# Partner rows land in three buffers and are added on VectorE, with the expert layers' gathers ordered by blocks of three

## The chip, the cores and the metric

The kernel runs on one core of one Trainium2 chip. The metric is the time of one launch on the device in microseconds (us). Engines are called PE (TensorE), DVE (VectorE), ACT (ScalarE), POOL (GpSimd) and SP (SyncE); PEld is PE's weight load. "Clock" is the TensorE clock that the chip granted, 1.0 being 2.4 GHz and 0.5 being 1.2 GHz.

## The reference, cut to what matters

Four layers follow each other on x of 4 x 1024 tokens of 128 numbers, each as `x = x + layernorm(layer(layernorm(x)))`: an attention over channels, a ternary feed-forward layer, a 16-head attention, and two expert layers. The change touches the last of them alone:

```python
xg = x.reshape(bsz, 4, n, d)...reshape(4, S, d)       # 4 groups of S = 1024 tokens
def per_group(xf, lw, lb):                            # E = 24 experts, top 2, C = 86 places
    combine, dispatch = top2_dispatch(xf, Wg, C)
    h = moe_apply(xf, combine, dispatch, W1, b1)      # 128 -> 512, a token's two experts summed
    h = relu(layer_norm(h, lw, lb))
    return moe_apply(h, combine, dispatch, W2, b2)    # 512 -> 128, summed again
return layer_norm(out + x, ln_out_w, ln_out_b)
```

A token sits in one place of each of its two experts. Its hidden row is the sum of two rows, one from each place, so each place needs the row of its partner place, and the token's result is again the sum of the rows at its two places.

## The kernel before, in words

The kernel is one program with its order written out by hand for each engine. Up to about 826 us of the profile stand the other layers; `expert_layers` is the rest. Work goes by group h (0 to 3). A group has 18 tiles of 128 places, in 6 blocks (NB) of 3 tiles (TPB) and 4 experts each. A block is numbered m or n, 0 to 23 over all groups; below, "block 2 of group 1" is m = 8.

The steps of a block are these.

- **Input.** POOL gathers token rows by index into one of the input buffers `XS` (`gather_x`, three gathers of 128 rows of 512 bytes). PE turns them (`x_transposes`, tile e_px), ACT copies (`xt`), PE multiplies by W1 (`up`, tile e_ph), ACT scales by the gate into `HS` (`hidden`, tile e_hs), and SP stores the three tiles to `h_rows` in HBM (`h_store`).
- **Partner.** When all 18 tiles of a group are stored (`h_out`), POOL gathers each tile's partner rows, 128 rows of 2 KB, and the DMA adds them onto `HS` in flight (`partners`, `ALU.add`).
- **Norm and second product.** ACT sums squares and takes the root (`std`), DVE scales the three tiles (`normed`), PE turns them in four chunks (`h_transposes`, tile e_pn), ACT applies relu into `HT` (`relu`), PE multiplies by W2 (`down`, tile e_py), DVE scales the result into `YS` (`result`) and SP stores it to `y_rows` (`y_store`).
- **Output.** Once a group's six results are stored, POOL gathers 16 tiles of result rows, 512 bytes each, into `YA` (`results`), and DVE adds them, normalises twice and adds to x (`output`); SP stores x (`x_store`).

While a group's second products run, PE also runs the first products of the next group: `beside(m)` puts one `up` behind each of the group's first four blocks, two behind the fifth and none behind the sixth. The last group has none. An `up(n)` starts with the transposes of block n+1. `pY` has two banks, so `down(m)` waits for `result(m-2)`.

Every gather goes through `gather`, which lets four be in flight: gather k waits for k-4 to have landed. `STAGES` numbers them in the order in which POOL issues them, and `landed` is how others wait for one. In group 0, DVE also works out the places of groups 2 and 3 (`choice.…`), with products on PE between its blocks (`map_products` behind `up(6)` and `up(7)`, which wait for `choice.spread`; `last_products` behind them, which wait for `choice.map_rows`).

The change touches `place` and `STAGES` (L1078 to L1088), the loops of SP, POOL, PE, ACT and DVE in `expert_layers` (L1713 to L2116), and the buffers at its head.

Of the kernel before, what the change touches and what calls it, by code (L numbers as in the profile page):

```python
# [13 lines left out]
P = 128  # L14
# [959 lines left out]
def exact_maxima(nc, R, S):  # L974

    with ExitStack() as ctx:
# [56 lines left out]
        def _(pe):  # L1033
# [39 lines left out]
NXS = 4  # L1073
# [4 lines left out]
STAGES = (("x", 0, 0), ("x", 0, 1), ("x", 1, 0), ("h", 0, 0), ("x", 1, 1), ("x", 2, 0), ("h", 1, 0), ("x", 2, 1), ("y", 0, 0),  # L1078
          ("x", 3, 0), ("h", 2, 0), ("x", 3, 1), ("y", 1, 0), ("h", 3, 0), ("y", 2, 0), ("y", 3, 0))
LENGTH = {"x": NT // 2, "h": NT, "y": 2 * GT}  # L1080
# [3 lines left out]
def place(stage, h, j):  # L1084

    if stage == "x":
        return FIRST[stage, h, 2 * j // NT] + j % (NT // 2)
    return FIRST[stage, h, 0] + j  # L1088
# [624 lines left out]
def expert_layers(nc, R, A, DR):  # L1713

    with ExitStack() as ctx:
# [8 lines left out]
        HT = [sb(f"e_ht{c}", [P, TPB * P]) for c in range(FC)]  # L1724
# [18 lines left out]
         sq_done, std_done, ov_done, od_done, out_done) = (sem("e_" + n) for n in (  # L1743
             "xt_mm", "xt_done", "h_mm", "hs_done", "n_done", "hn_mm", "ht_done", "y_mm", "ys_done",
             "ya_read", "o_done", "sq_done", "std_done", "ov_done", "od_done", "out_done"))
# [15 lines left out]
        def _(sp):  # L1761
# [12 lines left out]
            def x_store(h):  # L1774
                sp.wait_ge(o_done, h + 1)
                for b in range(B):
# [9 lines left out]
            for m in range(NU):  # L1786
                for n in beside(m):
                    h_store(n)
                y_store(m)
                if m == 3:  # L1790
# [7 lines left out]
                if m % NB == NB - 1 and m >= NB:  # L1798
                    x_store(m // NB - 1)
            x_store(GR - 1)  # L1800
# [3 lines left out]
        def _(pool):  # L1804
            token_numbers(nc, pool, R, W, 1)

            def inputs(h, first):
                pool.wait_ge(R["rows_done"], h + 1)
                if h == 2:
                    pool.wait_ge(R["x_out"], 16 * HB)  # L1810
                for n in range(h * NB + 3 * first, h * NB + 3 * first + 3):
                    if n >= NXS:
                        pool.wait_ge(xt_mm, n - NXS + 1)
                        gather_x(nc, R, n)

            def partners(h):
# [5 lines left out]
            def results(h):  # L1822
                for i in range(2):
                    pool.wait_ge(ys_out[i], (h + 1) * NB // 2 * 16)
                if h >= 1:
                    pool.wait_ge(ya_read, 2 * h)
                else:
                    pool.wait_ge(R["rows_done"], GR)
                for i in range(GT):
# [3 lines left out]

            inputs(0, 0)
            inputs(0, 1)
            inputs(1, 0)
            partners(0)
            inputs(1, 1)
            inputs(2, 0)
            partners(1)  # L1840
            inputs(2, 1)
            results(0)
            inputs(3, 0)
            partners(2)
            inputs(3, 1)
            results(1)
            partners(3)
            results(2)
            results(3)

        @block.tensor
        def _(pe):
# [11 lines left out]
            def up(n):  # L1864
                if n + 1 < NU:
# [26 lines left out]
            def down(m, c):  # L1892
# [10 lines left out]
                for e in range(EB):  # L1903
                    last = mm(out[0:ROWS, e * D:(e + 1) * D], HT[c][:, e * ROWS:(e + 1) * ROWS], W2[:, eb * EB + e, c, :],  # L1904
# [16 lines left out]
            for m in range(NU):  # L1921
                if m % NB == 0:
                    for c in range(FC):
                        h_transposes(m, c)
                for c in range(FC):
                    down(m, c)
                    if m % NB < NB - 1:
# [11 lines left out]
        def _(act):  # L1939
# [6 lines left out]
            def hidden(n):  # L1946
                if n + 1 < NU:
# [9 lines left out]
            def std(m):  # L1957
                for t in range(m * TPB, (m + 1) * TPB):
                    landed(act, R, place("h", t // NT, t % NT))
# [9 lines left out]
            def relu(m):  # L1969
                h = m // NB  # L1970
                for c in range(FC):
                    k = FC * m + c
                    act.wait_ge(hn_mm, k + 1)
                    if m >= 1:
                        act.wait_ge(y_mm, FC * (m - 1) + c + 1)
                    src = pN[k % 2][:, 0:TPB * P].rearrange("p (j s) -> p j s", j=TPB)
                    for cols, slots in ((slice(0, TPB * ROWS), slice(0, ROWS)), (slice(TPB * ROWS, EB * ROWS), slice(ROWS, P))):
                        r = nc.scalar.activation(HT[c][:, cols].rearrange("p (j s) -> p j s", j=TPB), src[:, :, slots],  # L1978
# [9 lines left out]
            for h in range(GR):  # L1988
# [4 lines left out]
                for j in range(NB):  # L1993
                    if j < 3:
                        std(m + j + (2, 2, 3)[j])
                    if j < NB - 1:
                        relu(m + j + 1)
                    if j == 1:
                        std(m + 4)
                    for n in beside(m + j):  # L2000
                        hidden(n)
            for n, eps in enumerate((R["c_ln_eps"], R["c_eps"])):
                act.wait_ge(ov_done, n + 1)
                nc.scalar.activation(or1, ov, ACT.Sqrt, bias=eps, scale=1.0 / D).then_inc(od_done, 1)

        @block.vector
        def _(v):
# [3 lines left out]
            group = lambda ap, h: ap.rearrange("p (b h r) d -> p b h r d", b=B, h=GR)[:, :, h, :, :]  # L2011

# [17 lines left out]
            def normalise(h, eps):  # L2030
                for i in range(GT):
                    c.mark(nc.vector.bn_stats(sto[:, i, :], Yn[:, i // 2 * TB + 2 * h + i % 2, :]))  # L2032
                c.wait()
                last = finish_stats(nc, c, sto, omean, ov, ot1, ot2, D)
                if h < GR - 1:
                    c.run(last)
                    rsqrt(nc, c, ov, or1, ot1, 1.0 / D, eps)
                else:
                    last.then_inc(ov_done, 1)
                    v.wait_ge(od_done, 1 if eps == LN_EPS else 2)  # L2040
                    c.run(nc.vector.reciprocal(or1, or1))
                for i in range(GT):
# [4 lines left out]
            def output(h):  # L2047
# [179 lines left out]
```

## Time and profile before

| | us |
|---|---|
| median of 3 runs (lowest, highest) | 1206.05 (1205.61, 1211.87) |
| profiled execution: its own time | 1214.45 |
| profiled execution: span | 1212.7 |
| busy in the span: PE, ACT, DVE, POOL | 910.2, 793.9, 562.8, 378.3 |
| expert layers, from 826 us to the end | about 387 |

From 800 us on no engine is busy throughout: PE is 45 of 50 us in 800 to 850, but 25.69 of 50 in 1000 to 1050 and 24.86 of 50 in 1100 to 1150. So what matters there is who waits for whom. The chain that ended last gives this: it is followed back from the last instruction, at each step to what released it. A timeline gives each instruction's start, its length, and in brackets the idle time of its engine before it with what ended it. Where several instructions stand on one line, "x3" counts them.

### The profile page before, as it was taken

The page shows a single profiled execution, that of the slowest core. Times are in us where ns is not written, and L with a number is a line of the kernel's source. Part 1 is how long each engine was busy: PE and PEld are TensorE (multiplying, and loading weights), DVE is VectorE, ACT ScalarE, POOL GpSimd, SP SyncE. Part 2 cuts the span into 40 slices and gives each one's busy share as a digit, 9 for nine tenths or more (in the row PEclk, how much of TensorE's full clock was granted, in tenths as well). Part 3 has the DMA queues.
Part 4 walks back from the last instruction along what each step waited for, and adds up shares of the span by engine and source line. Part 5 has one row for each costly group of instructions (what it writes and reads, how often), then busy time and mean ns, then how long its engine had stood idle before and what let it go on. Part 6 is the DMA issues. An engine that isn't in the chain of part 4 may idle for free. (4 is left out here: it accounts for less than half of the span.)

```text
span 1212.7 us, 18733 instructions
## 1 busy us (share of the span) xinstructions
PE 910.2 (75%) x6570; PEld 431.7 (36%) x6570; DVE 562.8 (46%) x1894; ACT 793.9 (65%) x1181; POOL 378.3 (31%) x333
## 2 busy tenths in 40 slices
PE   4746974661599999999999999998499496594740
PEld 4633762330122222222222223323276364463640
DVE  7488767894001444344445153334351225326356
ACT  2133351453699999999999999994476483574720
POOL 6222442543300000000000000115572766866752
PEclk9657996886699999999999999998699698698875
DMA  3000005647921111111112121238786874966821
GB/s 98 1 1 1 1 1 129 162 114 203 324 78 49 52 46 61 52 61 52 61 52 62 53 61 30 64 79 238 163 167 198 136 175 127 169 173 142 154 68 50
DMA packets 83615, 118.37 MB, mean 98 GB/s; under 512 B 8974, under 2 KB 45583, under 8 KB 83410
## 3 DMA queue, kind: packets, MB, share of 16 engines
q1 hardware_dynamic: 67344, 88.72, 24.2%
q0 software_dynamic: 14752, 27.81, 13.6%
q10 hardware_dynamic: 1442, 0.86, 0.3%
q8 instruction: 43, 0.70, 0.3%
q14 instruction: 34, 0.28, 0.1%
HBM read 72.66 MB, written 44.70 MB: 97 GB/s over the span
## 5 line engine op out<-in xcount | busy, mean ns | idle before, releaser
L1466 ACT ACTIVATE s_e<-s_ps 128x1024 f32<-128x1024 f32 x512 | 486.9, 1025 | 30.0 <-PE s_ps L1615 29.4
L1628 PE MATMUL s_acc<-s_e,s_v 128*32 128x512 f32 x2048 | 274.5, 608 | 0.1
L1615 PE MATMUL s_ps<-s_q,s_k 64*128 64x512 bf16 x1024 | 196.0, 389 | 50.2 <-ACT s_e L1466 22.6
L1100 POOL DMA_INDIRECT x_in<-x_tokens,rows_of x72 | 70.2, 976 | 502.2 <-DVE rows_of L1259 456.0
L1615 PEld LDWEIGHTS s_ps<-s_q,s_k 64*128 64x128 bf16 x1024 | 49.2, 93 | 320.7 <-ACT s_e L1466 274.8
L1100 POOL DMA_INDIRECT e_hs<-h_rows,rows_of x72 | 116.3, 1615 | 65.0 <-DMA h_rows<-e_hs 42.0
L1888 PE MATMUL e_pn<-ident,e_hs 128*128 128x128 f32 x288 | 54.1, 307 | 78.4 <-DVE e_hs L2018 57.3
L1904 PE MATMUL e_py<-w,e_ht 128*96 128x128 f32 x768 | 103.0, 282 | 0.0
L1978 ACT ACTIVATE e_ht<-e_pn,ln_hid 128x288 f32<-128x288 f32 x192 | 84.8, 507 | 26.7 <-PE e_pn L1888 26.7
L1904 PEld LDWEIGHTS e_py<-w,e_ht 128*96 128x96 f32 x768 | 92.5, 170 | 0.0
L1962 ACT ACTIVATE l_so<-e_hs 128x512 f32<-128x512 f32 x72 | 45.2, 628 | 65.1 <-DMA e_hs<-h_rows,rows_of 62.4
L1874 PE MATMUL e_ph<-w,e_xt 128*32 128x512 f32 x576 | 78.3, 617 | 5.7 <-ACT e_hs L1954 5.7
L1100 POOL DMA_INDIRECT e_ya<-y_rows,take x64 | 62.8, 981 | 27.6 <-issue 18.8
L1954 ACT ACTIVATE e_hs<-e_ph,gate_of 128x512 f32<-128x512 f32 x72 | 49.2, 687 | 31.0 <-PE e_ph L1877 30.3
L1888 PEld LDWEIGHTS e_pn<-ident,e_hs 128*128 128x128 f32 x288 | 38.3, 158 | 83.4 <-DVE e_hs L2018 44.4
L1548 DVE COPY s_as<-s_acc 128x512 f32<-128x512 f32 x32 | 22.1, 689 | 90.0 <-PE s_acc L1628 90.0
L1628 PEld LDWEIGHTS s_acc<-s_e,s_v 128*32 128x32 f32 x2048 | 40.4, 108 | 59.8 <-issue 56.0
L1566 DVE RECIPROCAL s_rec<-s_px 128x16 f32<-128x16 f32 x32 | 8.2, 258 | 114.8 <-PE s_px L1639 114.7
L2026 DVE TENSOR_TENSOR e_ys<-e_py,gate 96x512 f32<-96x512 f32 x24 | 16.3, 684 | 67.3 <-PE e_py L1904 67.3
L2016 DVE RECIPROCAL gate_exponents<-gate_exponents 128x3 f32<-128x3 f32 x24 | 4.2, 175 | 92.4 <-ACT gate_exponents L1966 92.4
L618 PE MATMUL f_pu<-f_zt,up_t 128*128 128x512 f32 x64 | 33.8, 663 | 9.8 <-ACT f_h L486 9.8
L500 POOL TENSOR_TENSOR f_sq<-f_sq 128x1024 f32<-128x1024 f32 x8 | 18.9, 2357 | 54.9 <-DVE f_sq L544 54.9
(413 smaller groups left out, 1334.9 us busy)
## 6 DMA issues: line engine op xcount, KB each, us to landing
h_rows<-e_hs SPq DMA_DIRECT2D x72, 256.0 KB, 3.1
s_k<-stack_k SPq DMA_DIRECT2D x32, 512.0 KB, 4.5
s_q<-stack_q SPq DMA_DIRECT2D x32, 256.0 KB, 3.2
w<-in_w SPq DMA_DIRECT2D x1, 6144.0 KB, 21.7
y_rows<-e_ys SPq DMA_DIRECT2D x24, 192.0 KB
stack_q<-b_parts SPq DMA_DIRECT2D x8, 384.0 KB, 4.5
stack_k<-b_parts SPq DMA_DIRECT2D x6, 384.0 KB, 4.3
x_res<-in_x SPq DMA_DIRECT2D x4, 512.0 KB, 7.3
```

What stands on the lines that cost most here:

```text
L618: mm(pU[f % 2][:], R["up_t"][:, f * P:(f + 1) * P], ZT[:, k * CH:(k + 1) * CH], start=True, stop=True).then_inc(up_mm, 1)
L1100: nc.gpsimd.indirect_dma_start(dst, None, rows, bass.IndirectOffsetOnAxis(ap=idx, axis=0), compute_op=op).then_inc(R["landed"][k % FLIGHT] ...
L1466: nc.scalar.activation(E[g % 4][:, 2 * pair:2 * pair + 2, :], pS[pair][:].rearrange("p (a s) -> p a s", a=2), ACT.Exp, scale=SCALE).then_i ...
L1548: nc.vector.tensor_copy(AS[hu % 2][:], acc[hu % 2][:]).then_inc(acc_read, 1)
L1615: last = nc.tensor.matmul(pS[pair][:, a * CH:(a + 1) * CH], K[c % 2][rows, pair, j * P:(j + 1) * P], Q[c % 2][rows, pair, :], start=True, ...
L1628: last = nc.tensor.matmul(acc[hu % 2][32 * h:32 * h + 32, :], V4[c % 2][:, j, h, :], E[g % 4][:, h, :], start=j == 0, stop=j == TB - 1)
L1874: mm(pH[m % 2][32 * q:32 * q + 32, :], XT[n % 2][:, j * P + 32 * q:j * P + 32 * q + 32], W1[:, e, :], start=True, stop=False)
L1888: tr = nc.tensor.transpose(pN[k % 2][:, j * P:(j + 1) * P], HS[:, m % NB * TPB + j, c * P:(c + 1) * P], ident[:])
L1904: last = mm(out[0:ROWS, e * D:(e + 1) * D], HT[c][:, e * ROWS:(e + 1) * ROWS], W2[:, eb * EB + e, c, :], start=False, stop=c == FC - 1, sk ...
L1954: nc.scalar.activation(HS[:, m % NT, :], pH[m % 2][:], ACT.Copy, scale=G128[:, n // NB, m % NT:m % NT + 1]).then_inc(hs_done, 1)
L1962: nc.scalar.activation(squares, HS[:, t % NT, :], ACT.Square, accum_out=ssq[:, t % NT:t % NT + 1]).then_inc(sq_done, 1)
L1978: r = nc.scalar.activation(HT[c][:, cols].rearrange("p (j s) -> p j s", j=TPB), src[:, :, slots], ACT.Relu, bias=lnh[:, 1, h, c:c + 1], sc ...
```

## The change

Six things change together. **Gathers of partner rows** no longer add: they land in one of three buffers `GA` (tile l_o, which is the old buffer `O`, and two new ones named e_ga), and DVE adds the buffer onto `HS` (`added`, one 128x512 addition a tile). A gather waits until the buffer's last addition is done. **POOL's order** goes by blocks: partner blocks and input blocks alternate after the first three partner blocks. **Input buffers** fall from four to three. **The transposes** of a group's first input block move from the last `up` of the group before to the start of the group, between `h_transposes` and `down` of its first block. **Results** are gathered, normalised and stored by halves of 4 tiles, and stand later: output of group 0 moves from group 1 to group 2, that of group 1 from group 2 to group 3, and that of group 2 from behind the last result to between the results of group 3. **ACT's** `std` and `relu` are reordered accordingly, and `std` waits for DVE's additions.

```diff
-NXS = 4
+NXS = 3
+NHT = 4
+NGA = 3
...
+        GA = [R["O"][:].rearrange("p t d -> p (t d)"), sb("e_ga1", [P, FF])[:], sb("e_ga2", [P, FF])[:]]
...
+            def partners(first, end):
+                h = first // NB
                 pool.wait_ge(h_out[h], 16 * NT)
-                for j in range(NT):
-                    gather(nc, R, place("h", h, j), HS[:, j, :], DR["h"][h].rearrange("t p f -> (t p) f"),
-                           IDX[:, h, 1, j:j + 1], ALU.add)
+                for j in range(first % NB * TPB, (end - h * NB) * TPB):
+                    t = h * NT + j
+                    if t < NGA:
+                        pool.wait_ge(R["late_mm"], (HB - 1) * NX + 1)
+                    else:
+                        pool.wait_ge(add_done, t - NGA + 1)
+                    gather(nc, R, place("h", h, j), GA[t % NGA], DR["h"][h].rearrange("t p f -> (t p) f"),
+                           IDX[:, h, 1, j:j + 1])
...
             def up(n):
-                if n + 1 < NU:
+                if n % NB < NB - 1:
                     x_transposes(n + 1)
...
             for m in range(NU):
-                if m % NB == 0:
+                h, j = m // NB, m % NB
+                if j == 0:
                     for c in range(FC):
                         h_transposes(m, c)
+                    if h + 1 < GR:
+                        x_transposes(m + NB)
...
+            def added(m):
+                for t in range(m * TPB, (m + 1) * TPB):
+                    landed(v, R, place("h", t // NT, t % NT))
+                    nc.vector.tensor_tensor(HS[:, t % NT, :], HS[:, t % NT, :], GA[t % NGA], ALU.add).then_inc(add_done, 1)
...
             for h in range(1, GR):
                 m = h * NB
-                for j in range(3):
-                    normed(m + j)
+                added(m)
+                added(m + 1)
+                normed(m)
+                added(m + 2)
+                normed(m + 1)
+                added(m + 3)
+                normed(m + 2)
                 result(m)
+                added(m + 4)
                 normed(m + 3)
                 result(m + 1)
+                added(m + 5)
                 normed(m + 4)
                 normed(m + 5)
+                if h == 3:
+                    output(1, 0)
                 for j in range(2, NB):
                     result(m + j)
-                    if j == 3 and h < GR - 1:
-                        output(h - 1)
-            output(GR - 2)
-            output(GR - 1)
+                    if h == 2 and j in (2, 4):
+                        output(0, j // 2 - 1)
+                    if h == 3 and j in (2, 4):
+                        output(j // 2, 2 - j // 2)
+            output(2, 1)
+            output(3, 0)
+            output(3, 1)
```

Three places show how instructions move; the prediction speaks of each.

DVE in group 0, before: from the last write of group 2's rows (`last_rows`, L1259) to the read of group 3's map (L1248). L1236 and L1238 are `spread(3)`, L2016 and L2018 `normed(3)`, L2026 `result(1)`.

```order
L1259 CAST rows_of<-e_pm 32x36
L1236 TENSOR_TENSOR v_all<-e_ya,v_all 128x1536
L1238 TENSOR_TENSOR v_all<-e_ya 128x1152
L2016 RECIPROCAL gate_exponents<-gate_exponents 128x3
L2018 TENSOR_SCALAR e_hs<-e_hs,gate_exponents 128x512 x3
L2026 TENSOR_TENSOR e_ys<-e_py,gate 96x512
L1248 COPY e_ya<-e_pm 96x72
```

The same place now; L2057 are the additions of blocks 4 and 5, L1242 and L1244 are `spread(3)`, L2072 is `result(1)`, L1254 reads the map.

```order
L1265 CAST rows_of<-e_pm 32x36
L2057 TENSOR_TENSOR e_hs<-e_hs,l_o 128x512
L2057 TENSOR_TENSOR e_hs<-e_hs,e_ga 128x512 x2
L1242 TENSOR_TENSOR v_all<-e_ya,v_all 128x1536
L1244 TENSOR_TENSOR v_all<-e_ya 128x1152
L2062 RECIPROCAL gate_exponents<-gate_exponents 128x3
L2064 TENSOR_SCALAR e_hs<-e_hs,gate_exponents 128x512 x3
L2057 TENSOR_TENSOR e_hs<-e_hs,l_o 128x512
L2057 TENSOR_TENSOR e_hs<-e_hs,e_ga 128x512 x2
L2072 TENSOR_TENSOR e_ys<-e_py,gate 96x512
L1254 COPY e_ya<-e_pm 96x72
```

The additions of block 5 now stand ahead of the map's read.

POOL from group 1's partners on, before: all 18 partner tiles in a row, then 9 tiles of input, 16 of results and 9 of input.

```order
L1100 DMA e_hs<-h_rows,rows_of 128x512 x18
L1100 DMA x_in<-x_tokens,rows_of 128x128 x9
L1100 DMA e_ya<-y_rows,take 128x128 x16
L1100 DMA x_in<-x_tokens,rows_of 128x128 x9
L1100 DMA e_hs<-h_rows,rows_of 128x512 x18
```

The end of group 1's stretch now, from its partner block 4 on; e_ya is half of group 0's results.

```order
L1106 DMA l_o<-h_rows,rows_of 128x512
L1106 DMA e_ga<-h_rows,rows_of 128x512 x2
L1106 DMA x_in<-x_tokens,rows_of 128x128 x3
L1106 DMA l_o<-h_rows,rows_of 128x512
L1106 DMA e_ga<-h_rows,rows_of 128x512 x2
L1106 DMA x_in<-x_tokens,rows_of 128x128 x6
L1106 DMA e_ya<-y_rows,take 128x128 x8
L1106 DMA x_in<-x_tokens,rows_of 128x128 x3
L1106 DMA l_o<-h_rows,rows_of 128x512
```

Partner gathers come in threes with three input gathers between them, and only 8 result gathers stand ahead of the next group.

DVE behind the last `normed` of group 3, before: the last four results (L2026) in a row, then the first additions of group 2's output (L2053, L2054).

```order
L2018 TENSOR_SCALAR e_hs<-e_hs,gate_exponents 128x512 x3
L2026 TENSOR_TENSOR e_ys<-e_py,gate 96x512 x4
L2053 TENSOR_TENSOR v_all<-v_all,e_ya 128x2x256
L2054 TENSOR_TENSOR v_all<-v_all,e_ya 128x2x256
L2053 TENSOR_TENSOR v_all<-v_all,e_ya 128x2x256
```

There now: the end of the first half of group 1's output, then block 2's result (L2072), then the start of the other half.

```order
L2092 TENSOR_SCALAR v_all<-v_all,gate_exponents 128x128 x4
L2112 TENSOR_TENSOR x_res<-x_res,v_all 128x2x256
L2072 TENSOR_TENSOR e_ys<-e_py,gate 96x512
L2101 TENSOR_TENSOR v_all<-v_all,e_ya 128x2x256
L2102 TENSOR_TENSOR v_all<-v_all,e_ya 128x2x256
L2080 BN_STATS gate_exponents<-v_all 128x6 x4
```

Each of block 2's to block 5's results now has a half of an output ahead of it or behind it.

## Rows read from the trace of the kernel before

**Rows 1.** chain that ended last, 740 to 1213 us, shares by line.
```profile
by line: POOL e_hs L1100 20.2%; issue 9.8%; PE e_ph L1874 7.9%; DMA e_hs<-h_rows,rows_of 6.7%; PE e_py L1904 6.5%; POOL e_ya L1100 6.2%; DMA h_rows<-e_hs 2.7%; DMA x_in<-x_tokens,rows_of 2.6%; PE e_pn L1888 2.4%; PE e_ph L1877 1.9%; PE e_px
```

**Rows 2.** timeline of POOL: start us, length us, line, what; idle before.
```profile
943.27 1.57 POOL L1100 DMA_INDIRECT e_hs<-h_rows,rows_of  x1 [17.73 <-DMA h_rows<-e_hs]
945.15 1.55 POOL L1100 DMA_INDIRECT e_hs<-h_rows,rows_of  x1 [0.30 <-issue]
1028.28 1.57 POOL L1100 DMA_INDIRECT e_hs<-h_rows,rows_of  x1 [5.27 <-DMA h_rows<-e_hs]
1105.78 1.57 POOL L1100 DMA_INDIRECT e_hs<-h_rows,rows_of  x1 [7.51 <-DMA h_rows<-e_hs]
```

**Rows 3.** timeline of ACT, group 1's start.
```profile
948.09 0.63 ACT L1962 ACTIVATE l_so<-e_hs 128x512 f32<-128x512 f32 x1 [9.46 <-DMA e_hs<-h_rows,rows_of]
959.57 1.70 ACT L1978 ACTIVATE e_ht<-e_pn,ln_hid 128x288 f32<-128x288 f32 x4
```

**Rows 4.** timeline of PE, group 1.
```profile
962.44 1.97 PE L1904 MATMUL e_py<-w,e_ht 128*96 128x128 f32 x8
1018.48 0.87 PE L1861 MATMUL e_px<-ident,x_in 128*128 128x128 f32 x3 [6.18 <-DMA x_in<-x_tokens,rows_of]
937.83 0.42 PE L1900 MATMUL e_py<-bias_split,expert_hot 128*96 128x128 bf16 x4
```

**Rows 5.** chain that ended last: PE's steady blocks, then two plain gathers landing.
```profile
916.67 0.90 PE e_py L1904 x8
925.54 0.90 PE e_py L1904 x8
1014.41 3.82 DMA x_in<-x_tokens,rows_of
1189.74 2.79 DMA e_ya<-y_rows,take
```

**Rows 6.** timeline of POOL, a plain gather of input rows.
```profile
1013.16 0.94 POOL L1100 DMA_INDIRECT x_in<-x_tokens,rows_of  x1 [0.30 <-issue]
```

**Rows 7.** timeline of DVE, scaling of three tiles.
```profile
953.99 1.28 DVE L2018 TENSOR_SCALAR e_hs<-e_hs,gate_exponents 128x512 f32<-128x512 f32 x3
```

**Rows 8.** windows: PE, PEld, DVE, ACT, POOL busy; PEclk, DMA share, GB/s.
```profile
950.00:956.00 6.00, 0.68 (x3) 0.68 (x4) 1.46 (x4) 2.46 (x7) 5.00 (x4) 0.50 0.87 136
```

**Rows 9.** timelines of PE and DVE in group 0.
```profile
873.88 1.51 PE L1888 MATMUL e_pn<-ident,e_hs 128*128 128x128 f32 x6 [13.50 <-DVE e_hs L2018]
907.37 0.42 PE L1900 MATMUL e_py<-bias_split,expert_hot 128*96 128x128 bf16 x4
884.78 1.74 DVE L1236 TENSOR_TENSOR v_all<-e_ya,v_all 128x1536 f32<-128x1536 f32 x1
886.45 1.34 DVE L1238 TENSOR_TENSOR v_all<-e_ya 128x1152 f32<-128x1152 bf16 x1
```

**Rows 10.** timelines of PE and DVE in group 3.
```profile
1123.13 1.54 PE L1888 MATMUL e_pn<-ident,e_hs 128*128 128x128 f32 x6 [17.67 <-DVE e_hs L2018]
1125.04 1.71 PE L1888 MATMUL e_pn<-ident,e_hs 128*128 128x128 f32 x6 [0.36 <-ACT e_ht L1978]
1139.44 0.69 DVE L2026 TENSOR_TENSOR e_ys<-e_py,gate 96x512 f32<-96x512 f32 x1 [0.79 <-PE e_py L1904]
```

**Rows 11.** timeline of DVE, last two output stages.
```profile
1168.61 1.64 DVE L2032 BATCH_NORM_STATS2 gate_exponents<-v_all 128x6 f32<-128x128 f32 x8
1173.65 2.14 DVE L2044 TENSOR_SCALAR v_all<-v_all,gate_exponents 128x128 f32<-128x128 f32 x8
1175.83 2.90 DVE L2060 TENSOR_TENSOR v_all<-v_all,gate_exponents 128x256 f32<-128x256 f32 x8
1186.06 1.23 DVE L2064 TENSOR_TENSOR x_res<-x_res,v_all 128x1024 f32<-128x1024 f32 x1
1192.65 0.69 DVE L2053 TENSOR_TENSOR v_all<-v_all,e_ya 128x512 f32<-128x512 f32 x1 [4.04 <-DMA e_ya<-y_rows,take]
1207.59 1.22 DVE L2064 TENSOR_TENSOR x_res<-x_res,v_all 128x1024 f32<-128x1024 f32 x1
```

More of the change, by code:

```diff
@@ L1772, in y_store, with x_store @@
                              ).then_inc(ys_out[m % 2], 16)
-            def x_store(h):
-                sp.wait_ge(o_done, h + 1)
-                for b in range(B):
+            def x_store(h, half):
+                sp.wait_ge(o_done, 2 * h + half + 1)
+                for b in range(2 * half, 2 * half + 2):
                     t = b * TB + 2 * h
@@ L1832, in results @@
                                take[:, h * GT + i, k:k + 1])
[L1834 to L1849, printed above, removed]
+            inputs(3, 9)
+            partners(0, 3)
+            inputs(9, 10)
+            partners(3, 4)
+            inputs(10, 11)
+            partners(4, 5)
+            inputs(11, 12)
+            partners(5, 6)
+            inputs(12, 15)
+            partners(6, 9)
+            inputs(15, 16)
+            partners(9, 10)
+            inputs(16, 17)
+            partners(10, 11)
+            inputs(17, 18)
+            partners(11, 12)
+            inputs(18, 20)
+            results(0, 0)
+            inputs(20, 21)
+            partners(12, 15)
+            inputs(21, 22)
+            partners(15, 16)
+            inputs(22, 23)
+            partners(16, 17)
+            inputs(23, 24)
+            partners(17, 18)
+            results(0, 1)
+            results(1, 0)
+            partners(18, 24)
+            results(1, 1)
+            for h in (2, 3):
+                results(h, 0)
+                results(h, 1)
         @block.tensor
@@ L1992, in _ @@
                 relu(m)
[L1993 to L1999, printed above, removed]
+                if h + 1 < GR:
+                    xt(m + NB)
+                for j in range(NB - 2):
+                    if j < 2:
+                        std(m + j + 2)
+                    relu(m + j + 1)
+                    if 1 <= j <= 2:
+                        std(m + j + 3)
                     for n in beside(m + j):
                         hidden(n)
-            for n, eps in enumerate((R["c_ln_eps"], R["c_eps"])):
-                act.wait_ge(ov_done, n + 1)
-                nc.scalar.activation(or1, ov, ACT.Sqrt, bias=eps, scale=1.0 / D).then_inc(od_done, 1)
+                relu(m + NB - 1)
+                for n in beside(m + NB - 2):
+                    hidden(n)
+            for half in range(2):
+                ts = slice(half * GT // 2, (half + 1) * GT // 2)
+                for n, eps in enumerate((R["c_ln_eps"], R["c_eps"])):
+                    act.wait_ge(ov_done, 2 * half + n + 1)
+                    nc.scalar.activation(or1[:, ts], ov[:, ts], ACT.Sqrt, bias=eps, scale=1.0 / D).then_inc(od_done, 1)
         @block.vector
```

112 lines of the change are left out of this document (60 added, 52 removed), and 3 rows, old and new, of the table STAGES.

## The prediction, written before the changed kernel had run

> **What bounds the kernel now.** I read the page's busy shares and slices first: behind 826 us no engine is full, so I turned to the chain that ended last for that stretch [rows 1]. A fifth of it is POOL writing the accumulating gathers (e_hs), 6.7% is their landing, the rest is PE work and the result gathers. The timelines show why. Each group has a handover: the last hidden tile is stored, POOL starts the partner gathers at 943.27, 1028.28 and 1105.78 in groups 1 to 3 [rows 2], and PE stands until the first blocks are normed. Call these starts G1, G2, G3. A group so lasts 85.0 us (G1 to G2), 77.5 (G2 to G3), and group 3 from G3 to the end of the span 106.9.
>
> **Prices.** An accumulating gather takes 1.55 us of POOL and 0.30 to the next [rows 2], and lands 4.8 us after its start (943.27 to ACT's 948.09) [rows 3]. A plain one of 512-byte rows takes 0.94 and 0.30 [rows 6] and lands 2.79 us after its start on a quiet chip, 3.82 beside other transfers [rows 5]. A plain gather of 2 KB rows is in no row. Its issue lies between 0.94 and 1.55; I take 0.95, since the number of rows is that of the plain ones and the accumulation is what goes. Its landing lies between 2.8 and 4.8; I take 3.3, half a microsecond above the quiet one for four times the bytes. A DVE addition of 128x512 is 0.69 [rows 11], about 0.72 apart. With three buffers, gather t+3 starts when t is added: 3.3 + 0.7 + 0.3 = 4.3 us a block, against 5.55 now. PE's steady block, second products and one `up`, is 8.87 us (916.67 to 925.54), the fifth block with two `up` 12.3 (to 937.83) [rows 4, 5].
>
> **Start of groups 1 to 3, from the gathers' start.** Now relu begins at +16.3 (959.57) [rows 3] and `down` of the first block at +19.2 (962.44) [rows 4]. Changed: third tile issued at 2.5, landed 5.8, added 6.5; block 1 added at 10.8. DVE has `added` of block 1 ahead of `normed` of block 0, so scaling (1.28 for three tiles [rows 7]) ends at 12.3. PE's transposes make relu possible at 13.3, `down` 2.9 later and 0.6 more for the moved input transposes: +16.8, a gain of 2.4.
>
> **Group 1.** `down` and `up` of the first block, as now 10.7 us, end at +27.5. POOL has per block three input gathers and three partner ones, 6 x 1.25 = 7.5 us, under PE's 8.87, but each input gather waits for transposes in the `up` three blocks earlier. Followed through: partner block 3 is added at +27, block 4 at +34.5. ACT has `std` of block 4 ahead of `hidden` of the second `up`, so that `up` loses 1.3. Block 5 is added at +43.3, in time within 0.2. So PE is at 27.5 + 3 x 8.87 + 1.5 = 55.6, the fifth block ends at +67.9, and 4.7 us later, as now, the next partner gathers start: 72.6 instead of 85.0. Of the 12.4 won, 2.4 is the start, 6.2 PE's wait for input rows at 1018.48, which stood behind 16 result gathers [rows 4], the rest small stalls of ACT. **Group 2** has the same sequence, and its outputs stand behind `added` and `normed`; the halves are hidden beside PE, whose two result banks suffice there. 72.6 against 77.5: 4.9 won.
>
> **Group 0 loses.** PE's first transposes are where they are now, 873.88 [rows 9]; with ACT not in the way the four chunks take 3.6 us as in group 3 (1123.13 to 1125.04 + 1.71) [rows 10], the input transposes 0.5: 878.0. Only then may POOL gather input block 9 (3.75 us) and behind it partner block 3: third tile started at +6.4, landed +9.7, added +10.5. DVE then does `normed(2)` (1.5) and `spread(2)` (3.1, [rows 9]), and `map_products` waits for that: it starts at 893.0 and PE gets to `down` of block 1 at 897. Second gate: the transposes of the following `up` end at 902.9, input block 11 and partner block 5 follow by the same 10.5, and DVE's map read stands behind `added` of block 5 and `result`: 914.4. `down` of block 2 starts at 915.2, now at 907.37 [rows 9]: 7.8 lost.
>
> **Group 3.** G3 is at 943.27 + 7.8 + 72.6 + 72.6 = 1096.2, 9.5 ahead of now. DVE comes 1.3 late to its additions, being in the last half of group 0's output. PE's first transposes are at +13.8, block 1's result 16.3 later (1123.13 to 1139.44) [rows 10], less 1.5 for stalls that go: +29; block 5 is added at 33 and the last `normed` ends at +36. From there DVE has no gap: four halves of output with the twelve-instruction root, five results of 0.7, two last halves. A whole stage now is 4 x 0.72 of additions, then 18.7 (1168.61 to 1186.06 + 1.23), of which 2 x 1.64 + 2 x 2.14 + 2.90 + 1.23 = 11.7 grows with the tiles [rows 11]. A half is 1.4 + 18.7 - 5.85 = 14.2; the small instructions aren't halved. The last group, with ACT's root, takes 16.2 from 1192.65 to 1208.8, so a half 16.2 - 5.85 = 10.4. Sum: 36.2 + 14.2 + 0.7 + 14.2 + 1.4 + 14.2 + 0.7 puts the last result at +81.6; its store and POOL's wake-up some 3.3 (as h_rows), eight gathers 10, landing: the second-last half could start at 96.5, and DVE is free at 95.8. So two halves of 10.4 end at +117.3, and the store takes the 3.9 of now (1208.8 to 1212.7): +121.2 against 106.9, 14.3 lost. PE isn't the bound: `down` of blocks 4 and 5 waits for results that stand behind half outputs. Queued behind each of DVE's waits for landed rows here are the results, and behind them SP's stores and POOL's last gathers.
>
> **At nothing.** Three instead of four input buffers: three transposes lie at least one 3.8 us `up` apart before group 0, as long as POOL's three gathers. x stores behind results on SP: two short DMAs that nobody waits for. `NHT` is 4 as before.
>
> **Sum.** +7.8 - 12.4 - 4.9 + 14.3 = +4.8 on the span of 1212.7. The profiled execution took 1214.45, 8.4 above the median, with 1.75 outside the span; the difference carries over: 1206.05 + 4.8, about 1210.8. Bounds: landing at 2.8 saves half a microsecond at each of some six places, -3; at 4.8 costs +9. Issue at 1.55 costs +20 (below). A measurement tells 0.5% (6 us) from no change.
>
> **A rule weighed.** POOL's plain gathers keep 0.94 in the stretch in which DVE's additions run [rows 6], though no row shows one beside a two-input DVE instruction held up or not. The Trainium skill, "SBUF — State Buffer", section "Who interferes with whom", says that a DVE instruction with two SBUF inputs contends with a GpSimd instruction that reads SBUF, not with one that only writes. `added` is 72 such instructions, and a gather reads its indices. By the rule each could hold a gather; the sum would become that of rival 2.
>
> **Rivals.**
> 1. *Issue stays at 1.55* because it goes with row size. A POOL block becomes 3 x 1.25 + 3 x 1.85 = 9.3 us, above PE's 8.87: the start loses 2.3 in groups 1 to 3, groups 1 and 2 some 5 more each, group 0's two gates 1.8 each: +20, 1231. For: nothing separates size and accumulation in these rows. Against: a gather of 128 rows is 0.94 whatever it fetches. It decides from 1.4 us on. Slower.
> 2. *Additions block the gathers.* Three times up to 0.7 in a block: 7.5 becomes 9.6, as rival 1, but half of the additions fall into POOL's waits: +12, 1218.
> 3. *The transfers get lighter.* The DMA engines are 0.87 busy while accumulating gathers run, moving 136 GB/s [rows 8]. If plain ones free them, group 0's gates open in time for PE (-7.8), landing is 2.8 (-3) and each of three handovers is 0.5 shorter: 4.8 - 12.3 = -7.5, 1198.5. Against: group 0's gates follow from the order, not from load.
> 4. *The halves don't bind.* If DVE's halves of output hid in group 3 as in group 2, its end would be as now, -14.3: 1196.5. The order of DVE speaks against it; I count it with 3.
>
> **Chances.** Forecast 0.50, own range 1203 to 1219, of which 0.30 within 0.5%, 0.16 slower, 0.04 faster. Rival 1 0.15, slower. Rival 2 0.12, slower mostly (0.01 within). Rivals 3 and 4 0.23, of which faster 0.21. Together faster 0.25, within 0.33, slower 0.42. Range 1196 to 1231: it leaves out about 0.1 on each side.
>
> **What would show it.** L1106 gathers into l_o and e_ga at 0.95 us, DVE's L2057 at 0.69 x72. From a group's first partner gather to the next one's about 73 us, twice. In group 0 PE idle ahead of `map_products` and again ahead of `last_products`, about 5 us. In group 3 PE idle before `down` of the last two blocks, DVE busy without gaps for some 80 us, and 121 us from G3 to the end. Wrong if POOL's issue is 1.5, if DVE has gaps in that last stretch, or if the group 0 waits on PE are missing.

## The result, and the profile after

The changed kernel takes 1249.19 us (median of 4 runs, 1246.36 to 1254.31), the kernel before on the same chip 1208.96 (4 runs): ratio 1.0335, 95% interval 1.0279 to 1.0391. It is slower by 40 us; 1210.8 was predicted, with a range up to 1231. The profiled execution has a span of 1249.5 us (1251.22 in all), 36.8 more than before.

The page of the changed kernel: busy time of each engine, the DMA queue of the gathers, the chain that ended last.

```profile
PE 918.9 (74%) x6570; PEld 443.5 (35%) x6570; DVE 627.5 (50%) x2092; ACT 794.9 (64%) x1183; POOL 339.1 (27%) x333
...
q0 software_dynamic: 10144, 27.81, 8.2%
...
issue 12%; POOL 8%; DVE 6%; DMA 5%; PE 3%; ACT 1%; POOLq 0%; DVEq 0%; ACTq 0%
```

POOL's busy time fell by 39 us and the gathers' queue from 13.6% to 8.2% of the DMA engines' time: what was taken away did go. No engine is full, as before; the time is in waits.

The stretches between the first partner gathers of the groups, as windows of the changed kernel (us; PE, PEld, DVE, ACT, POOL busy; granted clock; DMA share; GB/s). The last line is group 0's first partner gather in the kernel before:

```profile
857.30:959.00 101.70, 72.13 (x646) 55.28 (x646) 40.35 (x102) 51.15 (x115) 37.43 (x36) 0.80 0.45 136
959.00:1041.00 82.00, 58.34 (x522) 41.85 (x522) 24.60 (x48) 49.86 (x114) 45.11 (x44) 0.88 0.50 151
1041.00:1122.50 81.50, 59.93 (x522) 42.56 (x522) 45.47 (x145) 50.09 (x114) 42.88 (x44) 0.85 0.48 152
1122.50:1249.50 127.00, 38.88 (x289) 36.52 (x288) 99.65 (x380) 35.90 (x94) 58.97 (x58) 0.66 0.30 86
...
860.42 1.61 POOL L1100 DMA_INDIRECT e_hs<-h_rows,rows_of  x1 [11.52 <-DMA h_rows<-e_hs]
```

| stretch | before [rows 2] | predicted | after |
|---|---|---|---|
| G0 (860.42 before, 857.28 after) to G1 | 82.9 | 90.6 | 101.7 |
| G1 to G2 | 85.0 | 72.6 | 82.0 |
| G2 to G3 | 77.5 | 72.6 | 81.4 |
| G3 to the end | 106.9 | 121.2 | 127.0 |

**Prices.** Tiles e_ga and l_o in the changed kernel: the gather on POOL (min/median/max ns) and the median from issue to landing of each kind of gather.

```profile
L1106 POOL DMA_INDIRECT e_ga<-h_rows,rows_of x48: 947/953/3335, 858.5 to 1152.3; - x48
...
e_ya<-y_rows,take POOLq DMA_INDIRECT x64, 2.5
e_ga<-h_rows,rows_of POOLq DMA_INDIRECT x48, 4.1
x_in<-x_tokens,rows_of POOLq DMA_INDIRECT x45, 2.8
l_o<-h_rows,rows_of POOLq DMA_INDIRECT x24, 3.6
```

The issue is 0.953 us, as taken (0.95). Landing is 3.6 and 4.1 where I took 3.3. It varies: the addition of the first tile of groups 0 and 1 starts 3.3 and 3.5 us after its gather (857.28 to 860.57, 959.02 to 962.50), that of partner block 5 of group 0 only 5.6 us after (909.27 to 914.91).

**Group 0.** The two gates (the places where PE waits for DVE's map work) on POOL, PE and DVE. The last two lines are the start of `down` of block 2 and one of its four chunks:

```profile
888.85 3.33 POOL L1106 DMA_INDIRECT e_ga<-h_rows,rows_of  x1 [0.30 <-issue]
891.42 2.36 PE L1284 MATMUL e_pm<-v_all 128*96 128x72 f32 x13 [6.47 <-DVE v_all L1244]
905.50 0.95 POOL L1106 DMA_INDIRECT x_in<-x_tokens,rows_of  x1 [12.06 <-issue]
914.91 0.69 DVE L2057 TENSOR_TENSOR e_hs<-e_hs,l_o 128x512 f32<-128x512 f32 x1 [10.66 <-DMA l_o<-h_rows,rows_of]
918.15 0.22 DVE L1254 COPY e_ya<-e_pm 96x72 f32<-96x72 f32 x1
918.43 0.51 PE L1294 MATMUL e_pm<-e_ya,ident 96*32 96x18 f32 x6 [5.32 <-DVE e_ya L1254]
918.87 0.66 PE L1932 MATMUL e_py<-bias_split,expert_hot 128*96 128x128 bf16 x4
921.72 1.92 PE L1936 MATMUL e_py<-w,e_ht 128*96 128x128 f32 x8
```

And PE's granted clock ahead of the first `map_products`, in it, and in the other one:

```profile
885.00:891.40 6.40, 0.00 (x0) 0.00 (x0) 5.72 (x9) 3.03 (x8) 5.49 (x4) 0.68 0.80 206
891.40:897.20 5.80, 5.46 (x33) 5.26 (x34) 0.87 (x3) 0.00 (x0) 1.74 (x2) 0.50 0.45 135
910.10:913.20 3.10, 3.01 (x36) 2.79 (x32) 0.00 (x0) 0.69 (x1) 2.03 (x3) 1.00 0.88 269
```

The first gate opened at 891.42 (predicted 893.0; counted from G0 it is 1.5 us late, since G0 itself came 3.1 earlier). But PE had stood 6.47 us, and the granted clock of the products behind that wait was 0.50: they took 5.40 us instead of 2.94, and from their start to the input transposes of the next `up` PE took 12.85 us (891.42 to 904.27) where it had taken 8.66 (889.24 to 897.90). Then POOL, which had stood 12.06 us for the buffer of input block 11, could go on. Partner block 5 was added from 914.91 on, and the map's read came at 918.15 (predicted 914.4). `down` of block 2 started at 918.87 (predicted 915.2, before 907.37 [rows 9]): 11.5 us later than before, not 7.8.

From there to G1 PE took 40.1 us where it had taken 35.9. Block 2 alone took 5.0 us more (13.9 instead of 8.87): behind the wait of 5.32 us the chunks of `down` ran at half clock too (granted clock 0.50 from 918 to 922 us; 1.92 us for eight products instead of 1.04), about 2.9 us in all, and PE stood 1.91 us at 931.52 for a hidden tile from ACT. So G1 is 15.8 us later than before; the other 3.1 of the 18.9 in the table are G0, which came earlier by that much. As an estimate from these differences, 4.2 + 2.9 = 7.1 of the 15.8 us are half clock behind the two waits.

**Groups 1 and 2.** PE's waits in group 1 beyond the start, and the last addition of partner block 5 on DVE:

```profile
991.31 0.55 PE L1920 MATMUL e_pn<-ident,e_hs 128*128 128x128 f32 x3 [2.63 <-DVE e_hs L2064]
1000.47 1.06 PE L1906 MATMUL e_ph<-w,e_xt 128*32 128x512 f32 x8 [2.40 <-ACT e_hs L1989]
1012.25 1.07 PE L1906 MATMUL e_ph<-w,e_xt 128*32 128x512 f32 x8 [2.70 <-ACT e_hs L1989]
1009.47 0.69 DVE L2057 TENSOR_TENSOR e_hs<-e_hs,e_ga 128x512 f32<-128x512 f32 x1 [0.83 <-DMA e_ga<-h_rows,rows_of]
```

The wait for input rows at 1018.48 [rows 4] is gone. In its place PE waits for `normed` of block 2, which stands behind `added` of block 3, and twice for hidden tiles, which stand on ACT behind the statistics of blocks 4 and 5. The last additions of partner blocks 3, 4 and 5 ended at +30.8, +39.4 and +51.1 from G1, predicted +27, +34.5 and +43.3. Group 2 has the same waits (1.78, 3.91 and 1.91 us).

**Group 3.** DVE's last `normed` and the output behind it, the last result, the two waits of PE for result banks, POOL's last gathers, the last group's output. The first two lines are ACT's `relu` of block 3 and the root of block 5 behind it:

```profile
1157.70 2.50 ACT L2013 ACTIVATE e_ht<-e_pn,ln_hid 128x288 f32<-128x288 f32 x6
1163.62 0.30 ACT L2001 ACTIVATE gate_exponents<-gate_exponents,consts 128x3 f32<-128x3 f32 x1
1163.95 0.18 DVE L2062 RECIPROCAL gate_exponents<-gate_exponents 128x3 f32<-128x3 f32 x1 [4.63 <-ACT gate_exponents L2001]
1165.42 0.68 DVE L2101 TENSOR_TENSOR v_all<-v_all,e_ya 128x512 f32<-128x512 f32 x1
1210.09 0.68 DVE L2072 TENSOR_TENSOR e_ys<-e_py,gate 96x512 f32<-96x512 f32 x1
1180.52 0.66 PE L1932 MATMUL e_py<-bias_split,expert_hot 128*96 128x128 bf16 x4 [14.00 <-DVE e_ys L2072]
1195.49 0.66 PE L1932 MATMUL e_py<-bias_split,expert_hot 128*96 128x128 bf16 x4 [7.94 <-DVE e_ys L2072]
1214.09 0.95 POOL L1106 DMA_INDIRECT e_ya<-y_rows,take  x1 [21.63 <-DMA y_rows<-e_ys]
1225.65 0.69 DVE L2101 TENSOR_TENSOR v_all<-v_all,e_ya 128x512 f32<-128x512 f32 x1 [0.40 <-DMA e_ya<-y_rows,take]
```

DVE added block 5 by 1156.93 (+34.5, predicted 33), but its scaling starts at 1163.95, behind 4.63 us in which DVE stood: ACT's statistics of block 5 stand behind `relu` of block 3. From 1165.42 to 1210.7 DVE has no gap: three halves of some 14.4 us with the results between them, four in all. PE stands 14.0 and 7.9 us for banks that DVE has not read.

### The profile page after: what moved, and what is told of

It is laid out like the page before. It is cut to its first block and busy times, and to the rows that moved or that the text cites. A ratio compares the mean times of both kernels' runs of the same rounds, so it can differ in the third digit from the quotient of the medians.

```text
span 1249.5 us, 19008 instructions
## 1 busy us (share of the span) xinstructions
PE 918.9 (74%) x6570; PEld 443.5 (35%) x6570; DVE 627.5 (50%) x2092; ACT 794.9 (64%) x1183; POOL 339.1 (27%) x333
## 5 line engine op out<-in xcount | busy, mean ns | idle before, releaser
L1936 PE MATMUL e_py<-w,e_ht 128*96 128x128 f32 x768 | 110.8, 296 | 0.0
L1936 PEld LDWEIGHTS e_py<-w,e_ht 128*96 128x96 f32 x768 | 100.6, 182 | 0.0
L1554 DVE COPY s_as<-s_acc 128x512 f32<-128x512 f32 x32 | 22.0, 689 | 89.2 <-PE s_acc L1634 89.2
L1106 POOL DMA_INDIRECT e_ga<-h_rows,rows_of x48 | 50.9, 1060 | 19.9 <-issue 9.7
L2057 DVE TENSOR_TENSOR e_hs<-e_hs,e_ga 128x512 f32<-128x512 f32 x48 | 33.0, 692 | 33.3 <-DMA e_ga<-h_rows,rows_of 33.0
L2057 DVE TENSOR_TENSOR e_hs<-e_hs,l_o 128x512 f32<-128x512 f32 x24 | 16.5, 689 | 64.1 <-DMA l_o<-h_rows,rows_of 64.1
L2072 DVE TENSOR_TENSOR e_ys<-e_py,gate 96x512 f32<-96x512 f32 x24 | 16.2, 682 | 49.3 <-PE e_py L1936 49.1
```

Of the source, the lines that this page charges most:

```text
L1106: nc.gpsimd.indirect_dma_start(dst, None, rows, bass.IndirectOffsetOnAxis(ap=idx, axis=0), compute_op=op).then_inc(R["landed"][k % FLIGHT] ...
L1936: last = mm(out[0:ROWS, e * D:(e + 1) * D], HT[(FC * m + c) % NHT][:, e * ROWS:(e + 1) * ROWS], W2[:, eb * EB + e, c, :], start=False, sto ...
L2057: nc.vector.tensor_tensor(HS[:, t % NT, :], HS[:, t % NT, :], GA[t % NGA], ALU.add).then_inc(add_done, 1)
```

## The experiments

Ratios are to the kernel before on the same chip. The experiments ran on six chips. On three of them (told apart as "with gaps") the kernel before took 1283 to 1284 us instead of 1210, and every kernel traced there had ACT, DVE or both standing for up to 27 us where the trace names no instruction or transfer of this core that they waited for ("remote"). On the other chips the only such wait above 2 us is one of POOL near 192 us, 7.8 to 8.0 us long, far ahead of the expert layers. What is read from stretches comes from kernels without gaps, and a ratio with gaps is weak evidence: the same kernel differs by up to 3.6% between the two kinds of chip.

**Order of group 0** (ran beside the changed kernel again, 1.0336, G0 to G1 103.5).

```diff
-            partners(0, 3); inputs(9, 10); partners(3, 4); inputs(10, 11) ...
+            partners(0, 6)
+            inputs(9, 15)
```

> The changed kernel once more, unedited, so that the other kernels of this job have it beside them. Ratio to the kernel before 1.033 as in the first measurement if the chip plays no part; on the chip of the first job engines stood for 5 to 30 us at a time with nothing that they waited for, and if this job meets the same the ratio tells how much of the loss depends on that: between 1.01 and 1.05.

> The changed kernel with POOL's order of group 0 put back: all six partner blocks in a row, then input blocks 9 to 14. DVE's, PE's and ACT's orders as changed. Theory A (the gates of group 0 are set by input gathers ahead of partner ones): partner blocks 3 and 5 are added 10 us sooner, both waits of 12 us and more on POOL go, the span from the first partner gather of group 0 to that of group 1 falls from 101.7 to 85 to 90 us, the whole by 12 to 16 us against the changed kernel. Theory B (the chain of landing, addition and statistics in each block): POOL's row of 18 waits for additions as well, 4.6 to 5 us a block, and PE stands behind it; 101.7 falls by 5 us or less.

Measured: 1.0188 (1.0133 to 1.0242), 1234.9 us; G0 to G1 86.7 instead of 103.5. PE at the two gates of this kernel:

```profile
889.59 1.24 PE L1284 MATMUL e_pm<-v_all 128*96 128x72 f32 x12 [1.67 <-DVE v_all L1244]
904.15 1.24 PE L1284 MATMUL e_pm<-v_all 128*96 128x72 f32 x12
907.41 0.38 PE L1294 MATMUL e_pm<-e_ya,ident 96*32 96x18 f32 x6 [0.32 <-DVE e_ya L1254]
```

PE's two waits of 6.47 and 5.32 us have become 1.67 and 0.32, and the products take 2.94 at both. The granted clock is 1.00 from 880 to 910 us there. So 17 of the 40 us lost are POOL's input gathers ahead of partner gathers in this one group, the half clock behind its waits included.

**The same order in groups 1 and 2**: `partners(6, 12)` ahead of `inputs(15, 20)`, `partners(12, 18)` ahead of `inputs(21, 24)`.

> The changed kernel with POOL's partner blocks in a row in groups 0, 1 and 2, input blocks behind them; all else as changed. group0_in_a_row took 17 us off. Theory A (a partner block that stands behind an input block waits for PE's transposes, and ACT's statistics of blocks 4 and 5, with the hidden tiles queued behind them, wait for it): in group 1 of the changed kernel the last partner block is gathered at +42 to +45 and PE stands 2.4 and 2.7 us for hidden tiles; in a row it is through by +30, these stalls go, groups 1 and 2 take 76 to 78 instead of 80.5 and 82.5, in all 1225 to 1230 us. Theory B (landing and addition limit each block wherever POOL gathers it): both groups stay at 80 to 83, 1233 to 1237.

With gaps 0.9991, below what was expected (1225 to 1230 us of 1210). Measured again on a chip without:

> all_in_a_row again. Without gaps that nothing explains, group0_in_a_row had ratio 1.0188. Theory A: groups 1 and 2 take 76 to 78 us instead of 80.5 and 82.5, ratio 1.010 to 1.015. Theory B: 1.017 to 1.021.

Measured: 1.0145 (1.0098 to 1.0192). The windows of the four stretches, and PE's second wait for a hidden tile in group 1:

```profile
858.80:947.90 89.10, 67.37 (x646) 50.09 (x646) 40.40 (x102) 51.14 (x115) 39.79 (x36) 0.87 0.53 157
947.90:1024.90 77.00, 57.13 (x522) 40.64 (x522) 24.76 (x48) 49.66 (x114) 44.50 (x45) 0.87 0.52 159
1024.90:1101.00 76.10, 57.82 (x520) 41.33 (x521) 45.06 (x142) 49.54 (x114) 44.78 (x43) 0.87 0.51 162
1101.00:1228.00 127.00, 39.72 (x293) 37.24 (x291) 99.95 (x382) 35.90 (x94) 59.33 (x58) 0.66 0.30 86
...
997.48 1.07 PE L1889 MATMUL e_ph<-w,e_xt 128*32 128x512 f32 x8 [1.91 <-ACT e_hs L1972]
```

Groups 1 and 2 take 77.0 and 76.1, better than the 85.0 and 77.5 of before. PE's wait of 2.63 us for `normed` is gone, and those of 2.4 and 2.7 us fall to 1.91 each. By the stretches this is theory A (76 to 78); the ratio alone, at the upper end of A's range, would not tell it from B, since its interval reaches into B's.

**Outputs back at their places**, in two kernels: on the changed one, and on the one just told. DVE's part in the second:

```diff
-                if h == 3:
-                    output(1, 0)
                 for j in range(2, NB):
                     result(m + j)
-                    if h == 2 and j in (2, 4):
-                        output(0, j // 2 - 1)
-                    if h == 3 and j in (2, 4):
-                        output(j // 2, 2 - j // 2)
+                    if h < 3 and j in (2, 3):
+                        output(h - 1, j - 2)
+                    if h == 3 and j == 4:
+                        output(2, 0)
```

The gathers of result rows and the stores of x move with them. In the second kernel input blocks 18 and 19 also go behind the 16 result gathers of group 0, so this edit is more than DVE's order.

> The changed kernel with the outputs back at their earlier places: output of group 0 in group 1, of group 1 in group 2, the first half of group 2's between the results of group 3; all still by halves. Theory A: group 3 no longer has 2 x 14.4 us of group 1's output ahead of its results; the last result ends near +62 from the first partner gather of group 3 (it was +88), the end comes 39 us later: about 101 to 104 instead of 127.0, in all 1224 to 1230 us. Theory B: the last result is held by the chain of additions as well and ends at +72 or later: 1235 us or more.

The first kernel: 1.0268 with gaps (there the halves stood behind the fifth and sixth result). Its stretches can't be read; it decides nothing.

> in_a_row_outputs_early again. Theory A: group 3 takes 110 us instead of 127, ratio 0.996 to 1.003. Theory B: 1.005 or more, with PE waiting for result banks in groups 1 and 2 or a last result later than +72.

Measured: 1.0021 (0.9996 to 1.0046), 1212.1 us (with gaps 1.0008). Its last stretch, DVE's last `result`, and PE's wait at the start of group 2:

```profile
1099.30:1205.00 105.70, 34.00 (x288) 32.28 (x288) 77.03 (x273) 35.90 (x94) 52.58 (x50) 0.66 0.33 95
1165.69 0.68 DVE L2055 TENSOR_TENSOR e_ys<-e_py,gate 96x512 f32<-96x512 f32 x1
1035.35 1.54 PE L1903 MATMUL e_pn<-ident,e_hs 128*128 128x128 f32 x6 [20.00 <-DVE e_hs L2047]
```

105.7 instead of 127.0, the last result at +66.4 instead of +87.6; groups 1 and 2 give 6 us back (79.3 and 80.0; PE stands 20.00 us at the start of group 2, where it stood 14.81). No wait of PE for a result bank is left. With the two orders mended the loss is gone.

**Accumulating gathers in the new order**: no buffers, no `added`.

> accum_new_order again. If plain gathers are worth nothing and the order carries the loss, ratio 1.03 to 1.045 (the changed kernel has 1.0336). If landing and addition carry most of it, 1.005 to 1.015. The runs so far (1.0084 and 1.0033, with unexplained gaps) speak for the second; the three kernels of the second job speak for the first.

Measured: 1.0390 (1.0342 to 1.0438), 1256.2 us; with gaps it had been 1.0084 and 1.0033. The whole loss is there without a single plain gather. Groups 1 and 2 take 88.4 and 87.0 against 81.0 and 79.4 of the changed kernel on the same kind of chip: where input and partner blocks alternate, plain gathers are worth 7 to 8 us a group. Group 0 is the other way round, 91.9 against 103.5: no addition stands ahead of DVE's map reads, and PE waits 0.32 us for each of them, but 6.26 us at 908.26 for a hidden tile that stands on ACT behind the statistics of a late block.

**Plain gathers in the old order, and three input buffers alone.**

> The kernel before with only the plain partner gathers, three landing buffers and DVE's additions; POOL's order by groups, the transposes, whole results and the old places of the outputs stay. Input buffers are three, since four and the landing buffers don't fit together. Theory A (the order lost the time: group 0's gates and the outputs that moved into the last group): this kernel has neither, POOL is through its 18 partner rows some 6 to 9 us sooner, so the 6.2 us wait for input rows in group 1 goes: 1198 to 1210 us. Theory B (gather, landing, addition, statistics one behind another cost more than the accumulating gather, whatever the order): PE stalls in every group as it does in the changed kernel, 3 to 5 us a group: 1218 to 1228 us.

0.9965 (0.9945 to 0.9986), in theory A's range, but with gaps; this kernel was not measured without.

> The kernel before with three input buffers instead of four and nothing else. I had put this at nothing: ratio 0.998 to 1.002. If the buffers matter, POOL's nine input gathers in a row wait for transposes one `up` later each time: some 3 to 9 us, ratio 1.003 to 1.008, and then plain gathers are worth that much more than plain_old_order showed.

1.0017 (0.9991 to 1.0042): nothing that can be measured, as said. On the same chip plain gathers in the old order, with the two edits of the next paragraph, took 84.2, 82.3 and 78.1 for groups 0 to 2 and 61.3 to the last result, where three inputs alone took 83.5, 84.0, 78.2 and 59.1. In these two traces plain gathers win nothing in the old order.

**Halves, and roots on ACT.**

> The kernel before with results, outputs and stores by halves and nothing else; the outputs stay at their old places. Both theories price this alike: behind the last result DVE has two halves of 14.4 and two of 10.5, 49.8 us, where it had 20.2 + 6.7 of waiting for gathers + 16.2; so the end comes 5 to 7 us later: 1212 to 1216 us. If halves help by themselves (the last gathers overlap), it is 1203 to 1208.

1.0035 (1.0012 to 1.0058), with gaps; the last result to the end, a stretch without such a gap, took 53.0 instead of 47.5. Halves alone cost, as the sum of small instructions said. The next two kernels are the one with plain gathers in the old order and the kernel before, each with the same edit: group 2's output stays whole and takes its roots from ACT, and only group 3's goes by halves:

```diff
-                if h < GR - 1:
+                if h < GR - 2:
...
-            output(GR - 1)
+            output_half(GR - 1, 0)
+            output_half(GR - 1, 1)
```

> The kernel with the old order and plain gathers (plain_old_order) with two more edits behind the last result: the roots of group 2's output are taken by ACT as those of group 3's are, and group 3's results are normalised and stored by halves. From the rows: output of group 2 takes 20 - 2 x 2.9 = 14 us, the first half of the last one starts when its eight gathers have landed, some 17 us behind the last result, and two halves of 10.5 follow: last result to the end 41 us instead of 47.3. Ratio to the kernel before about 0.992 (0.9965 less 0.5%). If the halves only add small instructions, 0.996 or more.

0.9996 (0.9968 to 1.0025); the tail was 41.9 (expected 41), but the last result came later, and the whole was missed by 0.8%.

> root_old again: the kernel before with group 2's roots on ACT and group 3's results by halves. 0.9941 with the gaps; here 5.6 us of 1210, ratio 0.995 to 0.997.

0.9959 (0.9936 to 0.9982), 1204.0 us, and 0.9941 with gaps. This is 5 us below the kernel before, a small gain but clear of its interval. Its end: last result, start of group 2's output, start of the first half of group 3's.

```profile
1160.53 0.69 DVE L2032 TENSOR_TENSOR e_ys<-e_py,gate 96x512 f32<-96x512 f32 x1 [3.39 <-PE e_py L1909]
1161.14 0.68 DVE L2081 TENSOR_TENSOR v_all<-v_all,e_ya 128x512 f32<-128x512 f32 x1
1178.58 0.68 DVE L2061 TENSOR_TENSOR v_all<-v_all,e_ya 128x512 f32<-128x512 f32 x1
```

The output of group 2 takes 17.4 us instead of 21.4 (1165.84 to 1187.20 in the kernel before), and 41.9 pass from the last result to the end.

**Input block 18 ahead of the result gathers**, for PE's wait at 1018.48.

> plain_root with the gathers of input block 18 ahead of the sixteen result gathers of group 0 (they stood behind them). In plain_root PE waited 4.4 us for that block in group 1, and group 1 took 82.3 us. Without the wait 78 us; ratio to the kernel before 0.996 (0.9996 less 0.36%), 0.994 to 0.998. If the result gathers, now later, make DVE's output of group 0 run into group 2's additions, nothing is won: 0.999 or more.

1.0052 (1.0033 to 1.0071): slower. Group 1 took 77.8 as expected, but group 2 took 89.0:

```profile
1021.38 0.69 DVE L2098 TENSOR_TENSOR v_all<-v_all,e_ya 128x512 f32<-128x512 f32 x1 [9.34 <-DMA x_in<-x_tokens,rows_of]
1042.45 0.68 DVE L2034 TENSOR_TENSOR e_hs<-e_hs,l_o 128x512 f32<-128x512 f32 x1
1043.40 1.16 POOL L1105 DMA_INDIRECT l_o<-h_rows,rows_of  x1 [14.09 <-DVE e_hs L2034]
1052.50 1.33 PE L1905 MATMUL e_pn<-ident,e_hs 128*128 128x128 f32 x5 [30.23 <-DVE e_hs L2041]
```

The result gathers start at +50.0 of group 1 (997.97) instead of +45.1 in plain_root, so DVE's output of group 0 ends at +93 instead of +87, while the group itself is 4.5 us shorter. Group 2's additions stand behind it, and behind them POOL's landing buffers and PE. PE stood 30.23 us, twice its usual start. With accumulating gathers nothing of the next group stands behind the output:

> root_old with the gathers of input block 18 ahead of the sixteen result gathers of group 0. root_old has ratio 0.996; PE waits 7.7 us in its group 1 for that block (6.2 in the kernel before). Without the wait group 1 takes 77 to 79 us instead of 84.6: ratio 0.990 to 0.992, about 1198 us. If plain gathers were worth something by themselves, plain_input18_first would be at or below this; by the runs so far they are worth nothing or cost 2 to 4 us (first partner rows of groups 0 and 3), so it should be 3 to 6 us above.

0.9951 (0.9927 to 0.9975), with gaps, where 0.990 to 0.992 was expected and the same kernel without this edit had 0.9941 with gaps. The wait for input rows is gone, but no gain shows; without gaps it was not measured.

## Why the prediction was wrong

- **Prices**: right for issue (0.95) and addition (0.69). The landing was mis-sized: 3.6 and 4.1 us in the median, up to 5.7, not 3.3.
- **Group 0, +7.8**: the right mechanism, too small. G1 came 15.8 us later, and the stretch from G0 grew by 18.9. The step that failed is "7.8 lost": it has no term for PE's clock, and both waits it foresaw were followed by products at granted clock 0.50, some 7.1 us of the 15.8. Partner block 5 was added 4.1 us later than in the working, of which 1.9 are such late transposes, and a wait of 1.91 us for ACT behind the second gate was not in it. With its partner blocks in a row the group took 86.7.
- **Start of groups 1 to 3, a gain of 2.4**: none came. `down` of block 0 is at +19.1 (978.08) against +19.2. The slower landing is most of it: DVE ended scaling at +14.5 and not +12.3.
- **Groups 1 and 2, -12.4 and -4.9**: they came out at -3.0 and +3.9. "Block 5 is added at +43.3, in time within 0.2" is the step that failed: it was added at +51.1. Each input block ahead of a partner block waits for PE's transposes, a late partner block makes PE wait 2 to 3 us, and this makes the next transposes later. The wait of 6.2 us for input rows did go. With partner rows in a row over half of the predicted 17.3 us was there (77.0 and 76.1 against 85.0 and 77.5): the gather's issue was priced rightly and its place wrongly.
- **Group 3, +14.3**: +20.1. "The last `normed` ends at +36" is the step that failed: it ended at +43. Some 2 us are the late start; the rest is ACT, whose statistics of block 5 stand behind `relu` of block 3, an order that the working put at nothing (DVE stood 4.63 us for it). From 1165.42 to the end of the last result it took 45.4 as predicted, and from there to the end 39 (39.6). The text says five results where the sum rightly has four. It is the largest term, half of the loss, and foreseen in kind.
- **Rivals**: 1 is out (issue 0.95). For 2, 16 of 72 gathers took over 1.0 us, 7 us above the median in all; the longest, 3.33 us at 888.85, stands beside DVE's `spread`, and the kernel before has accumulating ones of 3.00 and 2.72 us beside the same instructions. With all 72 additions kept, putting the two orders back took the loss away (1.0021), so it isn't the cause. The trace of the kernel before could have told: at 1013.84 DVE adds two SBUF tiles of an output while POOL issues a gather from 1013.16 on, and that gather takes its 0.94 us. Its price of 12 us on 1210.8 should also have read 1222.8, not 1218. The Trainium skill, "SBUF — State Buffer", "Who interferes with whom", has a DVE instruction with two SBUF inputs contend with GpSimd's reads, and says in the same section that `tensor_tensor` was not seen to stall a DMA issued there; the median of 0.953 agrees with the second sentence. 3 is out, since the landing is longer than priced and both waits in group 0 are there; 4 is out by PE's waits of 14.0 and 7.9 us for result banks.
- **The sum**: the losses were taken one by one with the gains set against them in full. The gains of 17.3 us shrank to a loss of 0.9, and the range ended at 1231 because no case held two of the losses at once.

What stays open: group 0 takes 84.9, 86.7 and 89.2 us in three kernels with the same order there. In the slowest, PE stood 1.89 us at the first gate, its granted clock was 0.50 from 891 to 895 us, and about 3 us are this; in the other two the products took 2.94 us behind waits of 1.75 and 1.67 us. Why the clock fell in one and not in the others no run shows, nor where the 1.8 us between those two come from.

```profile
888.13 3.75 PE L1284 MATMUL e_pm<-v_all 128*96 128x72 f32 x32 [1.89 <-DVE v_all L1244]
```

## What to carry to other kernels

When a gather stream is put in order by need, look at what each transfer waits for: an input block whose buffer the consumer frees late must not stand ahead of rows that the same consumer needs now. Work moved to "later" on an engine that is idle now lands in the last stage, where nothing hides it; count that term by itself. A wait that an order brings can cost more than its length: here PE's clock was halved behind the two long ones. And a step that is in time by 0.2 us in a hand-made schedule is late.

## What the runs showed of the hardware

- A plain gather of 128 rows of 2 KB holds POOL for 0.953 us, as one of 512-byte rows; the accumulating one 1.55. It lands in 3.4 to 5.7 us (median 4.1), one of 512-byte rows in 2.5 to 2.8 in the median.
- The same 32 products took 2.94 us at granted clock 1.0 and 5.40 at 0.50, behind 6.5 us in which PE stood. Behind a wait of 1.89 us they once took 3.75, behind 1.67 and 1.75 us 2.94.
- On three chips the kernel before took 6% longer. In `root_old` there ACT stood 16.66 us and DVE 23.03 us with no releaser but "remote":

```profile
1027.93 0.91 ACT L1983 ACTIVATE e_ht<-e_pn,ln_hid 128x288 f32<-128x288 f32 x2 [16.66 <-remote]
1023.01 0.69 DVE L2032 TENSOR_TENSOR e_ys<-e_py,gate 96x512 f32<-96x512 f32 x1 [23.03 <-remote]
```

  Ratios between orders differed much there (accumulating in the new order 1.003 and 1.008, against 1.039). What causes the gaps was not tried.
